# Two mixture-of-experts stages: every expert on every token, or each token's rows copied to its experts' segments and worked off in blocks of 128

## The reference, cut to what matters

```python
combine = _route(x, router_weight, e_bias)          # [T, 32]: 8 weights per token, else 0
def body(acc, ws):
    wg, wu, wd, cw = ws
    h = jax.nn.silu(x @ wg.T) * (x @ wu.T)
    return (acc + cw[:, None] * (h @ wd.T), None)
acc, _ = jax.lax.scan(body, jnp.zeros_like(x), (Wg, Wu, Wd, combine.T))
shared = jax.nn.silu(x @ sWg.T) * (x @ sWu.T) @ sWd.T        # 352 units, all tokens
...
topk_w, topk_i = jax.lax.top_k(jax.nn.sigmoid(x @ gate_w), 6)   # second mixture
routed = jnp.einsum('tef,efd,te->td', act, wd, combine)
```

## Time and profile before

| | |
|---|---|
| median of 3 runs (lowest, highest) | 981.14 us (977.62, 983.72) |
| the profiled execution | 977.45 us |
| its span, first to last instruction | 975.7 us |
| mean granted TensorE clock | 0.948 of full speed |
| PE busy | 878.6 us, 90% |
| DVE, POOL, ACT busy | 760.2, 574.2, 532.4 us |

### The profile page before, as it was taken

One profiled execution on the slowest core, in us unless ns is written; L12 is line 12 of the kernel. 1 busy time (PEld: TensorE's weight loads), 2 busy tenths in 40 slices (PEclk: granted clock), 3 DMA queues, 4 the chain that ended last, 5 costly groups with the idle time before them and its releaser, 6 DMA issues.

```text
span 975.7 us, 16764 instructions
## 1 busy us (share of the span) xinstructions
PE 878.6 (90%) x6100; PEld 656.2 (67%) x6100; DVE 760.2 (78%) x1058; ACT 532.4 (55%) x936; POOL 574.2 (59%) x500
## 2 busy tenths in 40 slices
PE   5627777877999999999899999999999999999997
PEld 4525445545777777777676777777776777777775
DVE  5998788665888888877777677878878767878886
ACT  4527777644666666655446645444446654343432
POOL 4433766655899898976586565444347554334341
PEclk9868788678999999999999999999999999999999
DMA  5006999832776666642222122323322112232320
GB/s 192 2 1 136 179 176 164 160 97 55 145 152 143 142 152 151 148 125 68 78 66 81 51 66 83 95 86 94 97 82 82 57 58 82 82 91 87 97 87 22
DMA packets 162083, 97.79 MB, mean 100 GB/s; under 512 B 138833, under 2 KB 142801, under 8 KB 162001
## 3 DMA queue, kind: packets, MB, share of 16 engines
q1 hardware_dynamic: 161728, 96.19, 40.2%
q10 hardware_dynamic: 272, 0.52, 0.1%
HBM read 62.08 MB, written 1.05 MB: 65 GB/s over the span
## 4 chain that ended last, share of the span: by engine, by line
PE 65%; DVE 9%; POOL 6%; DMA 5%; issue 3%; ACT 3%; DVEq 0%; SPq 0%; POOLq 0%; ACTq 0%
PE psum L226 19%; PE psum L228 18%; PE psum L227 18%; DMA pT<-p 5%; PE psum L736 3%; DVE qstack L1441 2%; ACT e L1036 2%; POOL p L1491 2%; POOL wlo L1499 2%; PE psum L907 1%; PE psum L746 1%; PE psum L747 1%; DVE qstack L1427 1%; PE psum L893 1%; DVE nmax L1185 1%
## 5 line engine op out<-in xcount | busy, mean ns | idle before, releaser
L1499 POOL TENSOR_TENSOR wlo<-wraw,whi 128x768 fp32r<-128x768 f32 x146 | 272.2, 1864 | 196.9 <-ACT whi L1046 194.9
L226 PE MATMUL psum<-actT_hi,whi 128*128 128x512 f32 x584 | 244.3, 418 | 4.0 <-issue 2.1
L1148 ACT ACTIVATE h_hi<-qstack 128x512 fp32r<-128x512 f32 x146 | 92.5, 633 | 260.6 <-DVE qstack L1441 244.2
L228 PE MATMUL psum<-actT_hi,wlo 128*128 128x512 f32 x584 | 233.0, 399 | 0.0
L227 PE MATMUL psum<-actT_lo,whi 128*128 128x512 f32 x584 | 232.7, 398 | 0.0
L1441 DVE TENSOR_TENSOR qstack<-qstack 128x512 f32<-128x512 f32 x136 | 184.5, 1357 | 12.5 <-DVE qstack L1427 0.5
L1491 POOL TENSOR_SCALAR p<-e 128x1024 f16<-128x1024 f32 x128 | 142.7, 1115 | 84.4 <-ACT e L1036 68.7
L1036 ACT ACTIVATE e<-psum,nmax 128x1024 f32<-128x1024 f32 x128 | 142.6, 1115 | 42.7 <-DVE nmax L1185 28.7
L1185 DVE TENSOR_REDUCE nmax<-psum 128x1 f32<-128x1024 f32 x128 | 152.8, 1216 | 14.7 <-PE psum L736 12.1
L1419 DVE SCALAR_TENSOR_TENSOR qstack<-qstack,psum 128x512 f32<-128x512 f32 x146 | 99.8, 684 | 66.0 <-ACT qstack L1111 65.4
L226 PEld LDWEIGHTS psum<-actT_hi,whi 128*128 128x128 f32 x584 | 111.0, 190 | 36.5 <-issue 6.2
(11 more groups left out here) (196 smaller groups left out, 1148.0 us busy)
## 6 DMA issues: line engine op xcount, KB each, us to landing
wraw<-in_wffn SPq DMA_DIRECT2D x146, 384.0 KB, 3.1
pT<-p SPq DMA_TRANSPOSE x128, 2.9
ctxT<-in_ctxT SPq DMA_DIRECT2D x2, 512.0 KB, 5.1
x<-in_x SPq DMA_DIRECT2D x1, 1024.0 KB, 8.5
ctok<-in_ctx SPq DMA_DIRECT2D x1, 1024.0 KB, 11.1
out<-x SPq DMA_DIRECT2D x4, 256.0 KB, 2.9
kstack<-in_Wkv ACTq DMA_DIRECT2D x1, 512.0 KB, 5.0
kstack<-in_Wq SPq DMA_DIRECT2D x1, 256.0 KB, 8.7
```

The source lines that it names most:

```text
L226: pe.matmul(out, l_hi, r_hi, start=start, stop=False, **kw)
L228: return pe.matmul(out, l_lo, r_hi, start=False, stop=stop, **kw)
L1499: pool.tensor_tensor(wlo[:, g % RING, :], wraw[:, g % RING, :], whi[:, g % RING, :].bitcast(F32), ALU.subtract).then_inc(cf["w_lo"], 1)
```

## The change

Both mixtures are made over. Each token is computed for its own 8 (or 6) experts only.

- The routing gives a mask of the chosen experts, and a matmul with a triangle of ones (`rank`) ranks each token among those of its expert. A place in a table in device memory, `xs_dram`, follows: each expert has a segment of 1152 rows. POOL copies a tile's 128 rows of 288 numbers there with one indirect DMA for each choice: 8 tiles by 8 choices are 64 DMAs in the first mixture, 8 by 6 are 48 in the second (`scatter`).
- `tables` makes, for each block of 128 places, its row and its expert, in SBUF. SyncE writes 128 rows of zeros behind each expert's last row, 32 DMAs whose place is read from SBUF into a register (`pads_in`). The number of blocks is fixed: 95 and 79 (`BLOCKS`), whatever the counts.
- For each block SyncE reads row and expert from SBUF into registers (`value_load`) and loads the block's rows and, in the first mixture, that expert's down weights. PE reads the expert into a register too, and multiplies with a slice of the gate and up weights, which now all lie in SBUF. The result goes to a table `y_dram` by an indirect DMA from POOL, to the row `token * 8 + choice` (`y_scatter`).
- `routed_sum` loads each token's 8 (or 6) results and adds them with their weights to `x`.
- The splits into high and low parts are gone: all matmuls outside the first attention and the first block are plain fp32, one matmul where there were three.
- The first attention runs its 128 steps by itself; the second attention runs between the mixtures; neither lies beside a mixture now. The shared experts' units (24 and 16) run ahead of the blocks, beside routing and scattering.

```diff
+TOP = (8, 6)
+BLOCKS = tuple((T * k + EXPERTS * (P - 1)) // P for k in TOP)
+ROW = D + EXPERTS
+SEG = T + P
+XS_RING, Y2_RING = 4, 4
...
+                def block_in(n):
...
+                    if n >= XS_RING:
+                        sp.wait_ge(cf["xT_ps"], n - XS_RING + 1)
+                        sp.wait_ge(cf["idx"], n - XS_RING + 1)
+                    row = sp.value_load(tab[b:b + 1, 0:1], min_val=0, max_val=EXPERTS * SEG)
+                    sp.dma_start(xs[:, slot, :], xs_dram[layer][bass.DynSlice(row, P), :]).then_inc(xs_in[slot], 16)
+                    if layer == 0:
+                        if n >= XS_RING:
+                            sp.wait_ge(cf["down"], unit_of_block(n - XS_RING) + 1)
+                        e_ = sp.value_load(tab[b:b + 1, 1:2], min_val=0, max_val=EXPERTS - 1)
+                        rows = wffn[0][SHARED[0]:, :, 2 * D:].rearrange("j (e c s) n -> j e c s n", e=EXPERTS, s=2)
+                        for half in range(2):
+                            sp.dma_start(dn[half * TILES[0]:(half + 1) * TILES[0], slot, :, :],
+                                         rows[:, bass.DynSlice(e_, 1), :, half, :].rearrange("j e c n -> j (e c) n")
+                                         ).then_inc(dn_in[slot], 16)
...
+                def pads_in(layer):
+
+                    sp.wait_ge(cp["pad"], layer + 1)
+                    for i in range(EXPERTS):
+                        row = sp.value_load(pad_row[0:1, i:i + 1], min_val=0, max_val=EXPERTS * SEG - P)
+                        sp.dma_start(xs_dram[layer][bass.DynSlice(row, P), :], zeros[:, :]).then_inc(padded[layer], 16)
...
+                for s in range(STEPS):
                     turn(s)
+                sp.wait_ge(c2["exp"], STEPS)
+                for first in range(0, 28, 4):
+                    tiles_in(0, first, 4, cw["low"])
+                sp.wait_ge(c2["out_ps"], STEPS)
+                for first in range(28, TILES[0], 4):
+                    tiles_in(0, first, 4, cw["high"])
+                pads_in(0)
+                sp.wait_ge(cp["tab"], 1)
+                sp.wait_ge(padded[0], 16 * (EXPERTS + 1))
+                sp.wait_ge(scattered[0], 16 * NT * TOP[0])
+                for n in range(BLOCKS[0]):
+                    block_in(n)
+                layer_out(0)
+                for t in range(Y2_RING):
+                    sums_in(0, t)
...
+                def gate_up(q):
...
+                        e_ = pe.value_load(tab[index:index + 1, 1:2], min_val=0, max_val=EXPERTS - 1)
+                        of_block[q] = e_
+                        pe.wait_ge(cf["xT_sb"], n + 1)
+                        for k in range(KD):
+                            last = pe.matmul(out, xTs[:, n % 2, k, :], Wv[layer][:, k, :, :, bass.DynSlice(e_, 1), :],
+                                             start=k == 0, stop=k == KD - 1)
                     last.then_inc(cf["g_ps"], 1)
...
+                def ffn(layer, i):
+
+                    first, end = FIRST[layer], LAST[layer]
+                    q = first + i
+                    if q + 1 < end and routed(q + 1):
+                        x_block_transposed(q + 1)
+                    if q < end:
+                        gate_up(q)
+                    if first <= q - 1 < end:
+                        h_transposed(q - 1)
+                    if first <= q - 2 < end:
+                        down(q - 2)
...
+                def goes_to(q):
+
+                    n = block_no(q)
+                    layer, _, b, _ = units[q]
+                    dve.wait_ge(*landed(xs_in, n, XS_RING))
+                    step(dve.scalar_tensor_tensor(junk[:, 3, :], expert_no[:, :], block_expert[:, b:b + 1],
+                                                  xs[:, n % XS_RING, D:], ALU.is_equal, ALU.mult, accum_out=dot[:, 0:1]))
+                    step(dve.copy_predicated(idxf[:, b:b + 1], filled[:, b:b + 1], dot[:, 0:1]))
+                    if n >= XS_RING:
+                        dve.wait_ge(*landed(y_out, n - XS_RING, XS_RING))
+                    dve.tensor_copy(idxi[:, n % XS_RING:n % XS_RING + 1], idxf[:, b:b + 1]).then_inc(cf["idx"], 1)
...
+                def routed_sum(layer, u):
...
+                    for i in range(k):
+                        for t in two:
+                            last = dve.scalar_tensor_tensor(x[:, t, :], y2[:, t % Y2_RING, i * D:(i + 1) * D], wk[:, t, i:i + 1],
+                                                            x[:, t, :], ALU.mult, ALU.add)
...
+                def scatter(layer, g, some):
+
+                    pool.wait_ge(cp["placed"], 3 * layer + g + 1)
+                    for k, t in some:
+                        if k < TOP[layer]:
+                            pool.indirect_dma_start(
+                                xs_dram[layer][:, :], bass.IndirectOffsetOnAxis(posi[:, t, k:k + 1], 0), xaug[:, t, :],
+                                None).then_inc(scattered[layer], 16)
+
+                def y_scatter(q):
+
+                    n = block_no(q)
+                    pool.wait_ge(cf["y_sb"], n + 1)
+                    pool.wait_ge(cf["idx"], n + 1)
+                    slot = n % XS_RING
+                    pool.indirect_dma_start(
+                        y_dram[units[q][0]][:, :], bass.IndirectOffsetOnAxis(idxi[:, slot:slot + 1], 0), ybuf[:, slot, :],
+                        None).then_inc(y_out[slot], 16)
...
+                early = scatters(0)
+                for s in range(STEPS):
                     quantize(s)
...
+                    if s >= 106 and s % 2 == 0:
+                        scatter(0, 0, early[(s - 106) // 2:(s - 106) // 2 + 1])
+                scatter(0, 0, early[11:16])
+                norm_rstd(pool, step, 6, 3, cn[0]["stats"], cn[0]["rstd"])
+                scatter(0, 0, early[16:])
+                for g in (1, 2):
+                    scatter(0, g, scatters(g))
+                for b in range(BLOCKS[0]):
+                    y_scatter(unit_of_block(b))
```

More of the change, by code:

```diff
@@ L588, in build @@
[L588 to L591 removed]
+        UNITS, TILES = (176, 96), (44, 24)
+        PART_ROWS, PARTS = (88, 96), (2, 1)
+        SHARED = (3, 2)
+        GATE_SCALE = (2.5, 1.0)
+        STEPS = HEADS0 * NT
+        wffn = (a["wffn0"], a["wffn1"])
+        units = []
+        for layer in range(2):
+            for t in range(NT):
+                units += [(layer, "shared", t, part) for part in range(SHARED[layer])]
+            units += [(layer, "routed", b, 0) for b in range(BLOCKS[layer])]
@@ new lines, in item, with unit_shape, y_read @@
+        def item(q):
+            return sum(1 for i in range(q) if ends(i))
+        def unit_shape(q):
+            layer, kind, _, _ = units[q]
+            if kind == "shared":
+                return P, P, 1
+            return UNITS[layer], PART_ROWS[layer], PARTS[layer]
+        items = [q for q in range(len(units)) if ends(q)]
+        def y_read(i):
+            q = items[i]
+            if routed(q):
+                return cf["y_sb"], sum(1 for j in items[:i + 1] if routed(j))
+            return cf["x_sh"], sum(1 for j in items[:i + 1] if not routed(j))
@@ new lines, in build @@
+        padded = [sem(f"padded{i}") for i in range(2)]
+        scattered = [sem(f"scattered{i}") for i in range(2)]
+        cw = {n: sem("cw_" + n) for n in ("shared", "low", "high", "down1", "gu1")}
+        xs_in = [sem(f"xs_in{i}") for i in range(XS_RING)]
+        dn_in = [sem(f"dn_in{i}") for i in range(XS_RING)]
+        y_out = [sem(f"y_out{i}") for i in range(XS_RING)]
+        y_in = [sem(f"y_in{i}") for i in range(Y2_RING)]
+        cf = {n: sem("cf_" + n) for n in (
+            "xT_ps", "xT_sb", "g_ps", "s", "h", "hT_ps", "hT_sb", "down", "y_ps", "y_sb", "x_sh", "idx", "sum")}
@@ new lines, in rank @@
+                def rank(layer, g):
+                    t0, n = GROUP[g]
+                    pe.wait_ge(cp["mask"], 3 * layer + g + 1)
+                    ps = bank(group_bank(g))
+                    for i in range(n):
+                        t = t0 + i
+                        out = ps[:, i * EXPERTS:(i + 1) * EXPERTS]
+                        last = pe.matmul(out, before[:, :], mask[:, t, :], start=True, stop=t == 0)
+                        for j in range(t):
+                            last = pe.matmul(out, ones[:, :], mask[:, j, :], start=False, stop=j == t - 1)
+                    if g == 2:
+                        for t in range(NT):
+                            last = pe.matmul(ps[:, P:P + EXPERTS], ones[:, :], mask[:, t, :], start=t == 0, stop=t == NT - 1)
+                    last.then_inc(cp["rank_ps"], 1)
@@ new lines, in shared_out, with ffn @@
+                def shared_out(q):
+                    layer, _, t, _ = units[q]
+                    dve.wait_ge(cf["down"], q + 1)
+                    dve.scalar_tensor_tensor(x[:, t, :], bank(5 + item(q) % 2)[:, 0:D], tgate[:, 2 + layer:3 + layer], x[:, t, :],
```

(18 more changed lines are left out.)

1526 lines of the change are left out of this document (751 added, 775 removed).

## The result

The changed kernel takes 1374.91 us (median of four runs, 1369.32 to 1378.02), the kernel before 979.69 us in the same session: a ratio of 1.402, 95% interval 1.395 to 1.409. The forecast was 1155 us, range 1010 to 1310. The direction was right, and the time lies 65 us above the range.

What follows compares the result with a forecast made beforehand. PE's columns bound the mixtures before; the prediction summed nine stages, 83 + 214 + 83 + 394 + 27 + 66 + 79 + 171 + 36 = 1153, with 1.7 around the span 1155 us, range 1010 to 1310.

Steps and rivals of the forecast that it cites:

- the routing's 15 us: First attention, last 40 steps: routing of groups 0 and 1 on DVE, with 11 scatters, adds 15 us.
- POOL's scatters run beside this: Way to the first mixture's first block: scatters take 77 us, just hidden in the 83 us of this way.
- S: Price of one scatter on POOL, taken as 1.25 us from a possible 0.25 to 2.65.
- rival D: POOL bounds: a scatter costs 2.65 us, first blocks start 61 and 51 us later; 1305 us, chance 0.13.
- The ring: First mixture: row loads wait for down products of four blocks earlier; two blocks take 6.05 + 3R = 8.3 us.
- PE's iteration: First mixture, PE's work for one block: gate and up, down and four transposes, 2.65 us, plus its register R.
- Rival E: PE slower than its columns, by strided weights (1229 us) or a falling clock (up to 1360 us); chance 0.10.
- R: Time to read a register in the blocks and zero-row turns, taken as 0.75 us; called the likeliest way to be wrong.
- rival C: Faster: registers of 0.1 us and landings of about 1.8 let PE set the pace; 958 us, chance 0.10.
- four passes: Blocks' plain fp32 products cost about 3.8 times fp32r; gate and up, 2 x 352 columns, take 1.2 us.
- ACT bounds it: Second attention, now alone: ACT's work sets 3.3 us a pair, 16 pairs 53 us, 66 us in all.
- the second ring: Second mixture: a block's load follows `goes_to` of four blocks earlier; (5.0 + 2R)/3 = 2.17 us a block.

Runs made afterwards that it cites:

- Pacing by two: Against the changed kernel, each scatter of rows waits for the landing of the last but one, so two are under way; 1315.2 us, ratio 1.342.
- scatters later: Against the changed kernel, scatters wait until seven (second mixture: six) of eight tiles have their shared units; 1363.0 us, ratio 1.392.
- paced by one: Against the changed kernel, each scatter of rows is issued only after the one before has landed; 1436.3 us in one run.
- idle transposes: Against the changed kernel, PE runs six transposes of the identity before waiting for each first-mixture block's rows; 1315.8 us, ratio 1.344.

## Why the prediction was right in direction and wrong in size

**First attention, 34 us short.** The step of 1.52 us, timed from the 64 us stretch of the earlier trace rows, was nearly right. In the changed kernel the first 72 exponentials:

```profile
L1140 ACT ACTIVATE e<-psum,nmax x72: 1113/1113/1121, 86.6 to 197.7; 128x1024 f32<-128x1024 f32 x72
```

That is (197.7 - 86.6)/71 = 1.56 us a step, 5 us more over 128. The last 56 steps take from 197.7 to 319.6 us, 121.9 us. By 1.56 a step it would be 88; the routing beside them so costs 34 us, where the forecast had 15. Some 10 us more lie at both ends: the first exponential is at 86.6 and not at 83, and the attention ends 11 us after the last one. So the term that failed is the routing's 15 us. The stretch from 236 to 281 us held 17 steps, 2.6 us each, and a few of the routing's small instructions are slow there. Groups on DVE in that stretch (busy us, mean ns):

```profile
L1347 DVE TENSOR_TENSOR pairs<-pairs 128x32 f32<-128x32 f32 x1 | 1.1, 1062 | 0.0
...
L1348 DVE TENSOR_TENSOR pairs<-pairs 128x32 f32<-128x32 f32 x1 | 0.2, 177 | 0.0
```

1.06 us against 0.18 for the same form. This was read in the trace alone, and no run took it apart.

**Ways to the tables and first blocks, 35 + 12 and 38 + 8 us short.** The step that failed is "POOL's scatters run beside this". S was right and POOL does not bound, so rival D fell; but the sum priced the scatters for POOL's queue alone and left out what they do to the others. The zero rows cost 1.55 and 1.4 us each where the forecast had 1.15; undisturbed they take 1.14. Pacing by two took 38 us off the first way and 20 off the second. On the first way its tables come 36 us after the attention, where the forecast had 40. On the second they still come 56 us after it, not 36. With the scatters later or paced by one it is 47 and 43 us (the 50.5 and 46.4 above), so some 30 of the 38 us there are the scatters' too. The rest, which may be PE's clock or the routing, no run takes apart.

**95 blocks, 59 us short.** The ring is the cause of the pace, and its size at the full clock (8.03 for two) is within 4% of the forecast. The term that was mis-sized is PE's iteration in it. With PE's register the forecast had 2.65 + 0.75 = 3.4 us. At the full clock it takes 3.2 (615.28 to 618.47), but in the block behind the long wait 4.6 (632.09 to 636.70). Rival E named the half clock, with a chance of 0.10, and priced 0.82 throughout at 38 us and the half throughout at 200. The granted clock was 0.86, and idle transposes gave back 59. So E's price was too low as well: the clock is low just in the products that the ring waits for. The mistake was to keep E apart from the forecast. The forecast itself says that PE waits for DMA in each pair, and the earlier trace rows show what the clock does when PE waits, so the two belonged in one sum. The Trainium skill (TensorE: Matmul & The Clock Gate, "Why this matters for your kernels") warns of gaps between bursts. The gaps that it warns of are longer than this ring's, so the page alone does not give the 1360 us that the prediction took from it; here the products behind a gap of 2.30 us already took 2.71 us instead of 1.45.

**R, taken as 0.75, is 0.52.** With that the forecast's sum would give 6.05 + 3 x 0.52 = 7.6 us for two blocks, 33 us less over 95. The ring takes 8.03 because other parts are longer. SyncE's issues in that pair:

```profile
619.32 0.82 SPq L755 DMA_DIRECT2D dn<-in_wffn  x2
621.15 0.36 SPq L748 DMA_DIRECT2D xs<-xs_dram  x1
```

PE's down products end at 618.55. From there it is 0.77 us to the first issue, 0.82 for the two issues, 1.01 to the row's issue and 2.16 to PE's transposes at 623.31: 4.76 us, where the two reads (0.63 and 0.45), the issues (0.8) and the landing (2.6) of the forecast would be 4.5. PE's part, from 615.28 to 618.55, is 3.27 us, where 2.65 and a register of 0.48 would be 3.13. So it is luck that the blocks were short by just what the clock costs: too high an R covered what the ring holds beside its terms. The likeliest way to be wrong, as the prediction had it, was not where it went wrong. No run comes near the 0.1 us of rival C. The "four passes" hold: 1.45 us for two times 352 columns in four instructions, 1.2 forecast.

**Second attention, 33 us short.** "ACT bounds it" failed. First exponentials of steps two apart:

```profile
1003.79 0.47 ACT L1210 ACTIVATE W<-psum,a1nb 128x256 f32<-128x256 f32 x1 [3.23 <-DVE a1nb L1538]
...
1013.90 0.47 ACT L1210 ACTIVATE W<-psum,a1nb 128x256 f32<-128x256 f32 x1 [2.39 <-DVE a1nb L1538]
```

5.1 us a step, not 3.3, and ACT waits for DVE each time. The steps follow a chain PE, DVE, ACT, DVE, POOL, PE, which is longer than any engine's work; 16 x 1.8 = 29 us. The loads of the results behind the weights cost 8 us more; the two together are 4 us above the 33. Before the change other work lay over that chain. It was read in the trace. Whether the two buffers or PE's written order closes the chain was not tested.

**79 blocks and the tail** came as forecast (4 us off), the second ring of 2.17 us to the second decimal; with R at 0.52 it should have been 2.0, so its landing or a handshake is that much longer.

**In all** the span is 224 us above the sum. Runs show 125 of them: the clock in the blocks 59, what pacing by two takes off 58, the results behind the weights 8. Read in traces alone are some 25 for the chain of the second attention and 34 for the first attention, 19 of these the routing. The other 40 lie on the ways to the tables and first blocks (35), in the 79 blocks and the tail (4) and in rounding; the runs with scatters later or paced by one put part of the 35 on the scatters as well. That the measured 1375 us lie near the 1360 of rival E says nothing for E's half clock throughout.

## What to carry to other kernels

When a plan makes an engine wait regularly, put the half clock behind the wait into that same sum; behind a wait of 2.3 us PE's next four products took 1.3 us longer. Work that is taken out from under other work shows its latency, not its busy time: time such a stage by its chain, and by the whole stretch in which it already runs alone. Blocks chosen by registers need the loads issued ahead of every wait they don't depend on, and where indirect DMAs are issued back to back, try a limit on how many are under way: here it took off 60 us, though why is not known.

## What the runs showed of the hardware

- Useless transposes can pay: 546 of them took 59 us off, with the granted clock of the blocks from 0.86 to 0.99.
- While GpSimd issued indirect scatters (128 rows of 1152 bytes) 1.26 us apart, ScalarE, VectorE and PE stood still for 10 to 25 us at a time, and SyncE's read and issue of a zero row took up to 2.5 us instead of 1.14. This held also where the scatters' data moved as fast as they were issued. With at most two under way the longest wait on the way to the first tables fell from 15.2 to 9.3 us, at some 1.4 us a scatter.
- An indirect scatter of 128 rows costs GpSimd 0.96 us, to `xs_dram` and to `y_dram`, and back to back 0.30 more until the next starts.
- Reading a register from SBUF costs 0.63 us on SyncE (0.45 for the expert's, behind it) and 0.48 on PE. On PE it was free in the first mixture, as long as its queue was not late.
